# The last quarter of the third layer's sums, split by columns: 25 of 64 fields on the 120 columns that are there, the other 8 columns apart, and VectorE adding the parts

## The reference

```python
outs = []
for W, b in params:                       # three layers, cout = 128
    z = jnp.einsum('bhd,bfd->bhfd', x_vec, input)
    B, h, f, d = z.shape
    z = z.reshape(B, h * f, d)
    x_vec = jnp.einsum('oc,bcd->bod', W, z) + b[None, :, None]
    outs.append(x_vec.sum(axis=2))        # (512, 128)
return jnp.concatenate(outs, axis=1)      # (512, 384)
```

## Time and profile before

| | |
|---|---|
| median of 3 runs | 1118.36 us (1117.12 to 1119.52) |
| the profiled execution | 1118.71 us |
| its span, from the first to the last instruction | 1117.0 us |
| mean granted TensorE clock | 0.995 of full |
| TensorE busy | 1071.4 us, 96% |
| VectorE, ScalarE, GpSimd busy | 857.4, 717.8, 867.2 us |

### The profile page before, as it was taken

How to read it: one execution, slowest core, us unless ns; L and a number is a source line. 1 busy time by engine, 2 the same in 40 slices (tenths; PEclk the granted TensorE clock), 3 DMA queues, 4 the chain that set the end, 5 groups by cost and what they waited for, 6 DMA issues and landing times.

```text
span 1117.0 us, 17733 instructions
## 1 busy us (share of the span) xinstructions
PE 1071.4 (96%) x4781; PEld 804.3 (72%) x4781; DVE 857.4 (77%) x2518; ACT 717.8 (64%) x2433; POOL 867.2 (78%) x727
## 2 busy tenths in 40 slices
PE   4879999999999999999999999999999999999997
PEld 3767677777768777777778777777777877777676
DVE  5565788878794787888885788888887588887982
ACT  4456676767673676767674576766766477676781
POOL 3456898988985789897977679797988579799560
PEclk9999999999999999999999999999999999999998
DMA  6752423223231231423332133333222232321000
GB/s 253 200 120 76 93 76 73 77 55 95 64 86 53 51 98 52 97 71 81 88 67 58 45 85 83 67 94 75 77 57 74 57 74 77 73 76 46 1 22 8
DMA packets 108325, 85.87 MB, mean 77 GB/s; under 512 B 71040, under 2 KB 73824, under 8 KB 108096
## 3 DMA queue, kind: packets, MB, share of 16 engines
q1 hardware_dynamic: 105680, 73.98, 27.4%
q10 hardware_dynamic: 2544, 10.75, 2.8%
HBM read 14.75 MB, written 0.79 MB: 14 GB/s over the span
## 4 chain that ended last, share of the span: by engine, by line
PE 84%; DVE 7%; ACT 5%; issue 2%; DMA 1%; POOL 1%; ACTq 0%; DVEq 0%
PE y L875 57%; PE l L895 10%; PE l L875 7%; PE xt L986 5%; DVE acc L762 3%; PE l2p L998 3%; ACT prod L650 2%; ACT y L639 1%; DVE bd L718 1%; DMA gram<-in_L_rec_W_dram 1%; DVE acc L747 1%; DVE x1l L728 1%; DVE gram L835 1%; PE l2p L975 1%; ACT x1h L548 0%
## 5 line engine op out<-in xcount | busy, mean ns | idle before, releaser
L762 DVE SCALAR_TENSOR_TENSOR acc<-y,x0t,acc 128x128 f32<-128x128 f32 x1792 | 493.2, 340 | 69.3 <-PE y L875 63.2
L650 ACT ACTIVATE prod<-y,x0t 128x128 f32<-128x128 f32 x1280 | 368.9, 381 | 232.7 <-PE y L875 225.8
L875 PE MATMUL y<-w1h,x1h 128*128 128x512 f32 x1024 | 466.5, 456 | 13.9 <-DVE acc L762 11.8
L875 PE MATMUL y<-w1h,x1l 128*128 128x512 f32 x1024 | 402.4, 393 | 0.0
L875 PE MATMUL y<-w1l,x1h 128*128 128x512 f32 x1024 | 401.2, 392 | 0.0
L441 POOL TENSOR_TENSOR z<-z,xg 128x512 f32<-128x512 f32 (+2 forms) x272 | 372.6, 1374 | 14.2 <-DMA z<-xg 13.9
L451 POOL TENSOR_TENSOR pacc<-pacc,prod 128x512 f32<-128x512 f32 x192 | 253.0, 1318 | 138.5 <-ACT prod L650 138.5
L875 PEld LDWEIGHTS y<-w1h,x1h 128*128 128x128 f32 x1024 | 193.4, 189 | 115.9 <-issue 45.7
L639 ACT ACTIVATE y<-y,x0t 128x128 f32<-128x128 f32 x768 | 215.9, 350 | 74.0 <-PE y L875 73.9
L747 DVE TENSOR_TENSOR acc<-y,acc 128x512 f32<-128x512 f32 x192 | 132.6, 691 | 136.7 <-ACT y L639 133.1
L875 PEld LDWEIGHTS y<-w1l,x1h 128*128 128x128 f32 x1024 | 193.1, 189 | 59.1 <-issue 29.1
(11 more groups left out here) (93 smaller groups left out, 664.2 us busy)
## 6 DMA issues: line engine op xcount, KB each, us to landing
z<-xg SPq DMA_DIRECT2D x480, 128.0 KB, 2.4
w2t<-in_L_rec_W_dram ACTq DMA_DIRECT2D x8, 512.0 KB, 12.3
gram<-in_L_rec_W_dram ACTq DMA_DIRECT2D x8, 512.0 KB, 4.4
xg<-in_r_input_dram SPq DMA_DIRECT2D x30, 128.0 KB, 3.9
z<-xg SPq DMA_DIRECT2D x32, 96.0 KB, 2.5
z<-xg SPq DMA_DIRECT2D x15, 192.0 KB
gram<-in_L_rec_W_dram ACTq DMA_DIRECT2D x1, 2048.0 KB, 10.3
out_dram<-z SPq DMA_DIRECT2D x4, 192.0 KB, 1.9
```

Source lines behind the costliest of these rows:

```text
L650: last = nc.scalar.activation(prod[:, h % HSLOTS, k, :], y[c % YB][:, k * O:(k + 1) * O], ACT.Copy, scale=x0t[:, j, f:f + 1])
L762: ins = nc.vector.scalar_tensor_tensor(out=to, in0=of, scalar=x0t[:, j, f:f + 1], in1=b1r[:] if m == 0 else to, op0=ALU.mult, op1=ALU.add)
L875: ins = nc.tensor.matmul(to, stationary, moving, start=(first and k == 0), stop=(last and k == 2))
```

## The change

The last quarter's 64 fields are split. Fields 0 to 24 are taken apart by columns: for the 120 columns of the first 15 tiles they are added up in bank `y[0]`, 18 of them ahead of the last tile's `layer2` and 7 behind it; for the last 8 columns they are added up in bank `y[1]`, once ScalarE has copied them. Fields 25 to 63 run as before on all 128 columns in `l2`. VectorE copies the two parts into the place of the sums, and adds `l2` and the bias to them in one instruction, in place of ScalarE's `quarter_out`. The number of weight loads grows by those of 25 matmuls (50 passes).

```diff
--- before.py
+++ after.py
@@ -66,6 +66,7 @@
 QUARTER_PARTS = 8
 W_PARTS = 8
 QUARTER_AT = [CHUNKS + 2 + k for k in range(QUARTER_PARTS)]
+KNOWN_FIRST, KNOWN = 18, 25
 LOWER_AT = 4
 SUM_AT = 6
 
@@ -237,6 +238,8 @@
         l2p_made = sem("l2p_made")
         l2p_used = sem("l2p_used")
         l2_made = sem("l2_made")
+        l2_part_made = sem("l2_part_made")
+        tail_step = sem("tail_step")
         l2_used = sem("l2_used")
         sums_made = sem("sums_made")
         turned = sem("turned")
@@ -685,7 +688,6 @@
             upper(0, FIRST)
             groups(act, body)
             layer2_out(GROUPS * TILES - 1, (QG * TILES - 1) * TILE_B)
-            quarter_out(QUARTERS)
             row_out(B // P - 1)
 
 
@@ -860,6 +862,15 @@
             dve.wait_ge(l2p_made, layer2_ready(tile - 2))
             nc.vector.tensor_reduce(x2[:, slot], acc[:, slot].rearrange("p k o -> p o k"), AX.X,
                                     ALU.add).then_inc(x2_made, 1)
+            added_to = sums2_from_1[:, QUARTERS * QB:(QUARTERS + 1) * QB]
+            dve.wait_ge(l2_part_made, 1)
+            nc.vector.tensor_copy(added_to[:, 0:QB - TILE_B], y[0][:, 0:QB - TILE_B]).then_inc(tail_step, 1)
+            dve.wait_ge(l2_part_made, 2)
+            nc.vector.tensor_copy(added_to[:, QB - TILE_B:QB], y[1][:, 0:TILE_B]).then_inc(tail_step, 1)
+            dve.wait_ge(tail_step, 2)
+            dve.wait_ge(l2_made, QUARTERS)
+            nc.vector.scalar_tensor_tensor(out=added_to, in0=l2, scalar=b2d[:, 0:1], in1=added_to, op0=ALU.add,
+                                           op1=ALU.add).then_inc(l2_used, 1)
 
 
         @block.tensor
@@ -1072,9 +1083,27 @@
                             turn_fields()
 
             groups(pe, body)
-            layer2(GROUPS * TILES - 1, 1)
-            for part in range(QUARTER_PARTS):
-                quarter(QUARTERS, part, 2 * GROUPS)
+            known, rest = slice(0, QB - TILE_B), slice(QB - TILE_B, QB)
+            tile = GROUPS * TILES - 1
+            pe.wait_ge(l2p_used, tile + 1)
+            pe.wait_ge(acc_step, added(tile, CHUNKS - YB))
+            for f in range(KNOWN_FIRST):
+                nc.tensor.matmul(y[0][:, known], w2t[:, f, :], gram[:, f, known], start=(f == 0), stop=False)
+            layer2(tile, 1)
+            for f in range(KNOWN_FIRST, KNOWN):
+                last = nc.tensor.matmul(y[0][:, known], w2t[:, f, :], gram[:, f, known], start=False,
+                                        stop=(f == KNOWN - 1))
+            last.then_inc(l2_part_made, 1)
+            pe.wait_ge(l2p_used, tile + 2)
+            pe.wait_ge(prod_made, HN * tile + HN + HN)
+            for f in range(KNOWN):
+                last = nc.tensor.matmul(y[1][:, 0:TILE_B], w2t[:, f, :], gram[:, f, rest], start=(f == 0),
+                                        stop=(f == KNOWN - 1))
+            last.then_inc(l2_part_made, 1)
+            pe.wait_ge(x0t_made, 2 * GROUPS)
+            for f in range(KNOWN, F):
+                last = nc.tensor.matmul(l2, w2t[:, f, :], gram[:, f, :], start=(f == KNOWN), stop=(f == F - 1))
+            last.then_inc(l2_made, 1)
 
 
             turn_row(B // P - 1)
```

## The result

| | before | after |
|---|---|---|
| median of 13 runs | 1117.94 us (1116.31 to 1119.61) | 1121.00 us (1119.60 to 1122.89) |
| span of the profiled execution | 1117.0 us | 1120.2 us |

The ratio is 1.0028, with a 95% interval from 1.0020 to 1.0037: the change makes the kernel slower by 3.1 us. That is inside the predicted range, but the case forecast as likeliest was no change; what came is the first rival.

A forecast was written before the change was run, and what follows sets the result against it. A serial chain after the last tile bounds the end: +5.55 narrow passes, -3.02 earlier start, -1.35 products, -1.78 half clock avoided and small change give -0.47 us; forecast 1117.9 us, range 1116.2 to 1122.4.

The forecast's parts named there:

- the first rival: In the 8-column passes TensorE's clock falls to half: +1.2 to +4.8 us, around +3.5, or 1121.5 us; chance 0.38.
- The sum: Net change at the kernel's end with the clock full throughout: -0.47 us, giving 1118.24 against the profiled 1118.71.
- Start, 18 fields, products, 7 fields: TensorE's tail starts at 1091.95; 18 early fields end at 1096.06, last tile's products take 0.64 us, 7 more fields 1.55.
- the 0.1 set aside: Allowance in us, in all, for semaphore waits at the three changes of stretch in TensorE's tail.
- 120 and 8 columns cost as much as 128: Passes in the last quarter stay at 0.111 us at any width, since each loads 128x128 weights; 50 narrow ones take 5.55.
- the exposed 0.11: When a chunk starts from rest, its second weight load starts 0.11 us after the first; read as the load's own length.
- The cheap case: Rival: the 8-column passes take 0.063 us each, 3.15 in all, giving -2.9 us or 1115.5; chance 0.10.
- the estimate of 1.25 us: Time of the 50 8-column passes if only the skill's floor of about 25 ns per matmul counted; not the value adopted.
- ScalarE's copies covered, VectorE at the end: Seven fields hide ScalarE's copies, with 0.6 us of cover left; VectorE's final instruction takes 0.34 us, replacing ScalarE's 0.37.
- That the gain is a clock effect: Shorter TensorE idleness before the last quarter keeps the clock full; were it full before too, the change would lose 1.8 us.
- The price of the fall: Loss from half clock in the tail: 5.3 us if it falls 2 us into the narrow passes, 1.7 at their end.
- No effect of the clock in the timed runs: Rival: most timed runs before lack the clock fall, so time after is the forecast plus up to 1.5 us; chance 0.07.

## Why the prediction was wrong

The step that failed is the one on which the whole sum stood: "with TensorE idle for 0.4 us and not 3.4 the clock should not fall". The first half held: the clock did not fall from the gap at 1091.8. The second did not: it fell in the narrow passes, with no idle time. The prediction named that as its first rival and gave it 0.38 against 0.45, for want of a row on whether narrow passes count as work. The runs answer it: in stretches of 4.7 and 5.9 us (4.0 and 5.5 at full clock) the clock fell, in the same stretches at full width it did not, nor in the longer one mixed with wide passes. The sum had put such a fall at nothing; with 25 fields it cost 3.26 us in the tail (24.74 against 21.48 at full width). The sentence of the Trainium skill weighed there ("TensorE: Matmul & The Clock Gate", section "Loop structure matters more than you think") knows only gaps in which TensorE is idle. By it the clock would have held; the trace has it at 0.50 from 1104.6 to 1110.6 with TensorE busy throughout, and the measurement decides.

Point by point:

- *Start, 18 fields, products, 7 fields.* Right. 0.06 us of handoff; 4.21 us from there to the products (4.11 forecast); 0.64 (0.64); 1.55 plus 0.1 at the switch (1.55 and the 0.1 set aside).
- *120 and 8 columns cost as much as 128.* Right: 50 passes in 5.59 us at 128 columns, 50 in 5.65 at 32 (nearly all at full clock), and 36 in 4.21 less the first load at 120. The width of the moving side does not set the pass; that the weight load does is the prediction's reading of the exposed 0.11, which fits, but no run changed the load alone. The cheap case, at 0.063 a pass, is out. So is the estimate of 1.25 us by the floor of 25 ns in the Trainium skill ("TensorE: Matmul & The Clock Gate", section "Back-to-back issue gap"): the 50 passes took 5.65 us at 32 columns.
- *ScalarE's copies covered, VectorE at the end.* Right: the copies end at 1097.78, 0.9 us before the first narrow pass; VectorE's last instruction is 0.35 (0.34).
- *The sum.* -0.47 forecast for a full clock; the two kernels that have the full clock measure -0.20 by the tail and 1.0002 by the times. Of the 0.27 TensorE has 0.20, at the switches between stretches (0.2 and not 0.1) and by 0.112 in place of 0.111 a pass. The other 0.07 is a handoff that the sum took as alike: VectorE's last instruction starts 0.11 after TensorE's last pass ends (1111.67, 1111.78), ScalarE's in the kernel before 0.04 (1113.16, 1113.20).
- *That the gain is a clock effect.* Right, and shown by the filled idle time: 2.15 us in the tail against the 2.3 worked out. Splitting the fields without it is a loss, as worked out (1.8 us; 21.48 - 19.53 = 1.95 here).
- *The price of the fall.* The rival gave +1.2 to +4.8; it is +3.1. But its working had a wrong term: it took 3.4 us of wide passes until the clock is back, as in the earlier trace rows, and for a fall near the end of the narrow stretch a loss of 1.7 us. In the profile after, the fall came 0.8 us before the end of that stretch and 6.0 us of wide passes went by. The 3.44 us were not the whole of the half clock in the earlier trace rows: it lasted from 1093.6 to 1100.4, 6.8 us, and only the rest of it fell on the quarter's passes. After a fall in the narrow passes it lasted 6.8, 6.8 and 3.4 us (25 fields, 18 fields, 32 columns); why the third is shorter is open. That the total came near the rival's centre of +3.5 is partly luck: the fall came later than that centre supposes, and lasted longer.
- *No effect of the clock in the timed runs.* Out: filling the idle time takes 1.75 us off the median, so most timed runs of the kernel before have the fall.

## What to carry to other kernels

A pass of an fp32 matmul with its own 128-column weights cost 0.11 us here, however few columns it moved: splitting such a sum by columns pays for every pass twice. A long run of narrow matmuls can also lower TensorE's clock and slow down the wide ones behind it; moving the unused columns as well, or alternating narrow and wide, cost nothing here and avoided it. And where TensorE waits 3 us ahead of its last big piece, look at the granted clock of that piece first: filling the wait with matmuls whose results nobody reads was worth as much here (0.15%) as the best useful work found for it.

## What the runs showed of the hardware

- The clock fell with TensorE's records back to back: 5.1 us after the first of a run of passes of 8 columns, 3.1 us after it in another kernel, and 5.4 us after it with 32 columns. With passes of 8 and 128 columns in turn it stayed full for 13 us.
- Passes of 8, 32, 120 and 128 columns, each with its own weight load, are all 0.11 us apart at full clock.
- After the fall in the changed kernel, dense wide passes ran at half clock for 6.0 us before the clock rose, longer than the 3.44 us of the earlier trace rows. Counted from the fall, the half clock lasted 6.8 us in both, and 3.4 us in the execution with 32 columns.
- 28 passes whose results nobody reads, in TensorE's idle time, kept the clock full: the tail took 19.53 us against 21.68.
